# Attention row maxima: both heads' first factors in two row halves of the array, placed on either side of the P @ V batch

## The chip, the cores and the metric

The kernel runs on one core of a Trainium2 chip. The metric is the device time of one execution in microseconds (us). The engines are called as the profile calls them: PE is TensorE (PEld its weight loads), DVE is VectorE, ACT is ScalarE, POOL is GpSimd, SP is SyncE, which here issues all DMAs.

## The reference

For each of 16 images (256 channels, 32 x 32 positions): a group norm, self-attention with 4 heads of 64 channels over 1024 positions, a projection with a residual, and then a residual bottleneck of three convolutions whose weights are mixed from 8 experts per image.

```python
xn = group_norm(x, gn_w, gn_b)
q, k, v = split(einsum('oc,bchw->bohw', qkv_w, xn) + qkv_b[...])   # 4 heads of 64
attn = softmax(einsum('bhdm,bhdn->bhmn', q, k) / sqrt(64), axis=-1)
x = x + einsum('oc,bchw->bohw', proj_w, einsum('bhmn,bhdn->bhdm', attn, v)) + proj_b
rw = sigmoid(x.mean(axis=(2, 3)) @ router_w.T + router_b)
# conv 1x1 (256->64), conv 3x3 (64->64), conv 1x1 (64->256), weights einsum('be,e...->b...', rw, experts)
out = relu(conv3(relu(bn(conv2(relu(bn(conv1(x))))))) + x)
```

The softmax needs a number for each query that lies near the maximum of its row of scores; any such number gives the same result, since it cancels.

## The kernel before

Queries and keys are kept split into a first part (fp32r) and a small rest. `Q1[:, h]` holds the first part of head h's queries in both 64-partition halves; `K1[:, h]` holds the first part of the keys in one half and the rest in the other, so that a product over 128 partitions is q1 times (k1 + k2). `Q2` and `K2` hold the rest and, in one row, the negated row maxima with a row of ones.

An image is worked off as follows: a block is a pair of heads and a half of the queries (4 blocks), a step is one tile of 128 keys of a block (8 steps a block, 32 an image), a turn is two steps (`TURNS` = 16 an image). On PE a turn t is: the scores `S` of one step (`scores`, four matmuls, L541 and L544), the jobs of the table `MID` for this turn, the scores of the next step, the jobs of `LATE`, then both steps' P @ V products (`pv`, L557), then the jobs of `HALVES`. All jobs (QKV tiles, projections, convolutions, group-norm sums) share one PSUM bank, `SB`. ACT takes the exponential of each score tile and drains most banks, POOL adds up the probabilities, DVE reduces maxima, splits q and k, normalises and mixes the experts.

The row maxima are made one block ahead. A fill (`max_fill`, L522) writes the scores of 128 queries against all 1024 keys of one head into `MS` (two banks), two matmuls of 128 rows each; a `reduce_max` on DVE (L738) takes them down to one column of `mx`. `MS` exists once, so each fill waits on `max_read` for the reduce of the fill before it. A block has 8 fills (2 heads x 4 query tiles), a turn has 2: one after each step's scores. When a block's 8 columns are there, the job "row" (turns 2, 6, 10, 14; L470) transposes and negates them on PE, DVE copies them to `mrow` (L742), and SP sends them into `Q2`, where the block's scores need them (`rows_loaded`).

Each engine's program is written out in the same turn order and runs in that order; semaphores join them. So a PE instruction that waits holds all of PE behind it. `section` is emitted for images 0, 1, a loop body over images 2 to 14, and image 15; image 15 makes no fills after its own blocks.

## Time and profile before

| | |
|---|---|
| median of 3 runs | 2131.06 us (2130.21 to 2134.96) |
| the profiled execution | 2136.77 us, of which the span of the trace is 2135.0 us |
| busy share of the span | PE 92%, DVE 75%, POOL 52%, ACT 49%, PEld 50% |
| granted TensorE clock, mean | 0.988 |
| chain that ended last | PE 72%, DVE 17%, issue 8% |
| one image in the middle (turn 14 to turn 14) | 129.5 us |

A row of the profile's groups gives the line, engine and operation, what is written from what, the shapes, the count, then the busy time and the mean of one, then how long the engine sat idle just before and who ended the idle time. PE records last until a modelled end and overlap; the time from one start to the next is what a matmul costs in a stream.

### The profile page before, as it was taken

What the parts mean: (1) busy time and instruction counts of PE and PEld (TensorE: products, weight loads), DVE (VectorE), ACT (ScalarE), POOL (GpSimd) and SP (SyncE); (2) the same over time, 40 slices, a digit from 0 to 9 for tenths busy, and PEclk for the clock granted to TensorE, in tenths of its full rate; (3) what the DMA queues carried; (4) which work ended last, traced back from release to release, by engine and by line L of the source; (5) the groups of instructions that cost most, each with busy time, mean ns of one, the idle gap of its engine ahead of it and who ended that gap; (6) DMA issues with size and microseconds to landing.
All of it is one profiled execution on the core that took longest, in us unless ns stands there. A gap on an engine that the chain in (4) does not pass through costs nothing.

```text
span 2135.0 us, 26026 instructions
## 1 busy us (share of the span) xinstructions
PE 1960.0 (92%) x8072; PEld 1058.0 (50%) x8072; DVE 1598.7 (75%) x1750; ACT 1047.3 (49%) x1346; POOL 1112.6 (52%) x485
## 2 busy tenths in 40 slices
PE   5899899999999999899998999989999998999986
PEld 4455554545545445454454554545454554544532
DVE  5768868687785967959688686877859689596665
ACT  3554545454455454554445454544554545544432
POOL 2665545464564545545555554545645555455551
PEclk9999999999999999999999999999999999999998
DMA  4002120111202012020121201112020120201101
GB/s 150 21 21 70 26 89 21 48 47 25 89 20 86 8 35 79 20 94 10 30 74 25 89 17 42 55 25 89 20 85 10 35 79 20 94 10 30 54 6 65
DMA packets 44189, 102.02 MB, mean 48 GB/s; under 512 B 7168, under 2 KB 7936, under 8 KB 44032
## 3 DMA queue, kind: packets, MB, share of 16 engines
q1 hardware_dynamic: 44160, 101.65, 15.6%
q8 instruction: 16, 0.26, 0.1%
q14 instruction: 13, 0.11, 0.0%
HBM read 37.91 MB, written 16.78 MB: 26 GB/s over the span
## 4 chain that ended last, share of the span: by engine, by line
PE 72%; DVE 17%; issue 8%; ACT 2%; DMA 1%; DVEq 0%; SPq 0%; POOL 0%; ACTq 0%
PE PV L557 17%; PE SB L428 11%; PE S L541 9%; PE MS L522 9%; PE S L544 7%; DVE mx L738 5%; PE SB L465 5%; PE SB L499 4%; DVE rz L807 3%; PE SB L507 3%; PE SB L459 3%; DVE mix L830 2%; PE SB L486 2%; DVE gsc L721 1%; DVE bst L715 1%
## 5 line engine op out<-in xcount | busy, mean ns | idle before, releaser
L414 POOL TENSOR_TENSOR psum_p<-psum_p,prob 128x1024 f32<-128x1024 f32 x384 | 933.0, 2430 | 658.5 <-ACT prob L620 652.4
L738 DVE TENSOR_REDUCE mx<-MS 128x1 f32<-128x1024 f32 x500 | 604.3, 1209 | 312.6 <-PE MS L522 309.3
L620 ACT ACTIVATE prob<-S 128x1024 f32<-128x1024 f32 x512 | 523.6, 1023 | 383.1 <-PE S L544 380.8
L557 PE MATMUL PV<-prob,V 128*64 128x512 f32 x2048 | 503.1, 613 | 0.0
L541 PE MATMUL S<-Q,K 128*128 128x512 f32 x1024 | 457.2, 446 | 3.0 <-DVE mx L887 3.0
L544 PE MATMUL S<-Q,K 128*128 128x512 f32 x1024 | 404.1, 395 | 0.0
L522 PE MATMUL MS<-K,Q 128*128 128x512 f32 x1000 | 330.0, 411 | 68.2 <-DVE mx L738 68.2
L541 PEld LDWEIGHTS S<-Q,K 128*128 128x128 f32 x1024 | 192.8, 188 | 261.6 <-issue 217.3
L414 POOL TENSOR_TENSOR psum_p<-prob 128x1024 f32<-128x1024 f32 x64 | 154.3, 2411 | 308.4 <-ACT prob L620 308.4
L557 PEld LDWEIGHTS PV<-prob,V 128*64 128x64 f32 x2048 | 125.9, 138 | 262.4 <-issue 238.6
L522 PEld LDWEIGHTS MS<-K,Q 128*128 128x128 f32 x1000 | 175.5, 189 | 159.7 <-DVE mx L738 130.0
L807 DVE RECIPROCAL rz<-rz 128x256 f32<-128x256 f32 x128 | 222.7, 1740 | 3.2 <-ACT rz L649 2.3
L544 PEld LDWEIGHTS S<-Q,K 128*128 128x128 f32 x1024 | 193.8, 189 | 38.0 <-issue 10.8
L775 DVE TENSOR_TENSOR K<-qk_raw,K 64x512 fp32r<-64x512 f32 x128 | 107.0, 836 | 85.8 <-ACT K L638 84.9
L775 DVE TENSOR_TENSOR Q<-qk_raw,Q 64x512 fp32r<-64x512 f32 x128 | 124.7, 974 | 50.1 <-ACT Q L638 49.2
L634 ACT ACTIVATE qk_raw<-SB,vec 128x512 f32<-128x512 f32 x124 | 85.4, 689 | 81.8 <-PE SB L428 80.7
L830 DVE SCALAR_TENSOR_TENSOR mix<-ex,rw,mix 128x768 f32<-128x768 f32 x105 | 118.7, 1131 | 1.4
L465 PE MATMUL SB<-o,wp 128*128 128x512 f32 x240 | 112.7, 592 | 0.0
L625 ACT ACTIVATE o<-PV 128x512 f32<-128x512 f32 x64 | 38.3, 598 | 141.3 <-PE PV L557 141.3
L428 PE MATMUL SB<-x_hi,w_hi 128*128 128x512 f32 x248 | 98.7, 398 | 4.3 <-DVE x_lo L730 4.3
L428 PE MATMUL SB<-x_lo,w_hi 128*128 128x512 f32 x248 | 98.1, 395 | 0.0
L428 PE MATMUL SB<-x_hi,w_lo 128*128 128x512 f32 x248 | 97.9, 395 | 0.0
(126 smaller groups left out, 1929.7 us busy)
## 6 DMA issues: line engine op xcount, KB each, us to landing
xin<-in_x_dram SPq DMA_DIRECT2D x16, 1024.0 KB, 6.5
K<-K SPq DMA_DIRECT2D x128, 128.0 KB, 2.3
Q<-Q SPq DMA_DIRECT2D x128, 128.0 KB, 2.2
x<-in_x_dram SPq DMA_DIRECT2D x16, 1024.0 KB, 5.1
out_dram<-y SPq DMA_DIRECT2D x64, 256.0 KB, 2.0
V<-v_next SPq DMA_DIRECT2D x16, 512.0 KB, 4.4
hpad<-hpad SPq DMA_DIRECT2D x16, 289.0 KB, 3.1
ex<-in_experts_dram SPq DMA_DIRECT2D x1, 3072.0 KB, 11.9
```

The costliest lines, as they stand in the source:

```text
L414: nc.gpsimd.tensor_tensor(acc, first_in, prob[:, s % PBUF, :, :], ALU.add).then_inc(add_done, 1)
L428: last = nc.tensor.matmul(dst, wl(w, c), xl(m, c), start=(k == 0), stop=(k == 3 * CC - 1))
L465: last = nc.tensor.matmul(bank, wp[:, c, oc * P:oc * P + P], o[:, c, px(hf)], start=(c == 0), stop=(c == CC - 1))
L522: last = nc.tensor.matmul(MS[:, nh, :], Q1[:, h, q0:q0 + P], K1[:, h, px(nh)], start=True, stop=True)
L541: nc.tensor.matmul(S[:, s % 2, a, :], K1[:, h, kt * P:kt * P + P], Q1[:, h, px(hf)], start=True, stop=False)
L544: last = nc.tensor.matmul(S[:, s % 2, a, :], K2[:, h, kt * P:kt * P + P], Q2[:, h, px(hf)], start=False, stop=True)
L557: last = nc.tensor.matmul(PV[own(a), :], V[:, b // NH, kt, a * D:a * D + D], prob[:, s % PBUF, a, :], start=(kt == 0), stop=(kt == KT - 1))
L620: nc.scalar.activation(prob[:, s % PBUF, :, :], S[:, s % 2, :, :], ACT.Exp, scale=D ** -0.5).then_inc(exp_done, 1)
L738: nc.vector.reduce_max(mx[:, b % 2, m:m + 1], MS[:, :, :], AX.XY).then_inc(max_read, 1)
L775: last = nc.vector.tensor_tensor(dst, qk_raw[own(a), f % 2, :], hi[own(a), h, px(hf)].bitcast(F32), ALU.subtract)
L807: nc.vector.reciprocal(rz[:, f % 2, cols], rz[:, f % 2, cols]).then_inc(rz_ready, 1)
L830: nc.vector.scalar_tensor_tensor(out=mix[:, :], in0=ex[:, e, :], scalar=rw[:, e:e + 1], in1=mix[:, :], op0=ALU.mult, op1=ALU.add).then_inc ...
```

## The change

A fill now writes both heads' scores for 128 queries and one half (512) of the keys: head a's matmul uses only the 64 partitions that hold its first parts (`own(a)`: rows 0 to 63 of the array for head 0 of the pair, rows 64 to 127 for head 1) and writes bank a of `MS`. The rest of the keys is left out of the maximum. There are still 8 fills a block and 2 a turn. In PE's program both leave their places behind the scores: one stands directly before the turn's P @ V products, the other behind these and the `HALVES` job. In DVE's program both reduces stand together behind the `LATE` jobs of the turn. A reduce now gives two columns (one for each head), for one key half; a ninth, small reduce for each block takes the larger of the two halves, and `row` waits for that one (`max_ready`).

```diff
-        mx = sb("mx", [P, 2, 2 * QT])
+        mx = sb("mx", [P, NH, 2, QT])
+        mx1 = sb("mx1", [P, 2 * QT])
...
-                    pe.wait_ge(max_read, 8 * (BLOCKS * i + f + 1))
-                    last = nc.tensor.matmul(bank[0:2 * QT, 0:P], mx[:, f % 2, :], negeye[:, :], start=True, stop=True)
+                    pe.wait_ge(max_ready, BLOCKS * i + f + 1)
+                    last = nc.tensor.matmul(bank[0:2 * QT, 0:P], mx1[:, :], negeye[:, :], start=True, stop=True)
...
                 pe.wait_ge(max_read, 32 * i + 8 * b + m)
-                q0 = hf * HALF + m % QT * P
-                for nh in range(NH):
-                    last = nc.tensor.matmul(MS[:, nh, :], Q1[:, h, q0:q0 + P], K1[:, h, px(nh)], start=True, stop=True)
+                q0 = hf * HALF + t * P
+                for a in range(2):
+                    last = nc.tensor.matmul(MS[:, a, :], Q1[own(a), 2 * p + a, q0:q0 + P], K1[own(a), 2 * p + a, px(nh)],
+                                            start=True, stop=True)
                 last.then_inc(max_filled, 1)
...
                             scores(i + 1, half)
-                        at = fill_at(i, 2 * t + half, last)
-                        if at:
-                            max_fill(*at)
                         for kind, di, f in jobs_of(place, t, first, last):
                             job(kind, i + di, f, held)
                             held = [(kind, i + di, f)]
+                    at = fill_at(i, 2 * t, last)
+                    if at:
+                        max_fill(*at)
                     pv(i, 2 * t)
                     pv(i, 2 * t + 1)
                     for kind, di, f in jobs_of(HALVES, t, first, last):
                         job(kind, i + di, f, [] if kind == "conv2" else held)
                         held = [(kind, i + di, f)]
+                    at = fill_at(i, 2 * t + 1, last)
+                    if at:
+                        max_fill(*at)
...
+            def max_of(g, b, m, banks):
+
+                dve.wait_ge(max_filled, g + 1)
+                nc.vector.reduce_max(mx[:, m % NH, :, m // NH], banks, AX.X).then_inc(max_read, 1)
+
+            def max_of_block(i, b):
+                dve.wait_ge(max_read, 32 * i + 8 * b + 8)
+                wait(dve, filled["row"], BLOCKS * i + b)
+                nc.vector.reduce_max(mx1[:, :], mx[:, :, :, :].rearrange("p n a t -> p (a t) n"), AX.X).then_inc(max_ready, 1)
+
             def max_reduce(i, b, m):
-                n = 32 * i + 8 * b + m + 1
                 if m == 0:
-                    wait(dve, filled["row"], BLOCKS * i + b - 1)
-                dve.wait_ge(max_filled, n)
-                nc.vector.reduce_max(mx[:, b % 2, m:m + 1], MS[:, :, :], AX.XY).then_inc(max_read, 1)
+                    wait(dve, max_ready, BLOCKS * i + b)
+                max_of(32 * i + 8 * b + m, b, m, MS[:, :, :])
+                if m == 7:
+                    max_of_block(i, b)
...
                     for half, place in ((0, MID), (1, LATE)):
-                        at = fill_at(i, 2 * t + half, last)
-                        if at:
-                            max_reduce(*at)
                         for kind, di, f in jobs_of(place, t, first, last):
                             job(kind, i + di, f)
+                        if half == 1:
+                            for n in (2 * t, 2 * t + 1):
+                                at = fill_at(i, n, last)
+                                if at:
+                                    max_reduce(*at)
```

The twelve fills ahead of image 0 (`max_fill_pair`) change in the same way and stay where they are.

On PE, in turn 7 of the loop body (a turn without jobs), the end of the turn before the change reads as follows; L544 is the last of the turn's scores, L522 the fill, L557 the P @ V products, L541 the next turn's first scores.

```order
L544 MATMUL S<-Q,K 128x512
L519 REGISTER_ALU
L522 MATMUL MS<-K,Q 128x512 [waits max_read]
L522 MATMUL MS<-K,Q 128x512
L557 MATMUL PV<-prob,V 64x512 [waits exp_done]
L557 MATMUL PV<-prob,V 64x512
L557 MATMUL PV<-prob,V 64x512 [waits exp_done]
L557 MATMUL PV<-prob,V 64x512
L541 MATMUL S<-Q,K 128x512 [waits exp_done]
```

After the change (L546, L523, L559 and L543 are the same operations) it reads:

```order
L546 MATMUL S<-Q,K 128x512
L520 REGISTER_ALU
L523 MATMUL MS<-K,Q 128x512 [waits max_read]
L523 MATMUL MS<-K,Q 128x512
L559 MATMUL PV<-prob,V 64x512 [waits exp_done]
L559 MATMUL PV<-prob,V 64x512
L559 MATMUL PV<-prob,V 64x512 [waits exp_done]
L559 MATMUL PV<-prob,V 64x512
L520 REGISTER_ALU
L523 MATMUL MS<-K,Q 128x512 [waits max_read]
L523 MATMUL MS<-K,Q 128x512
L543 MATMUL S<-Q,K 128x512 [waits exp_done]
```

The fill that stood behind the turn's first scores (not in these rows) has gone, one stands before the P @ V products and one stands behind them, each with its wait for the reduce of the fill before.

On DVE, in turn 9 of the loop body (a QKV job for Q in `MID` and one in `LATE`), the order before is this; L738 is the reduce of a fill, L775 the split of q for a head.

```order
L738 TENSOR_REDUCE mx<-MS 128x1 [waits max_filled]
L773 ISA
L775 TENSOR_TENSOR Q<-qk_raw,Q 64x512 [waits qk_hi]
L773 REGISTER_ALU
L775 TENSOR_TENSOR Q<-qk_raw,Q 64x512 [waits qk_hi]
L737 REGISTER_ALU
L738 TENSOR_REDUCE mx<-MS 128x1 [waits max_filled]
L773 ISA
L775 TENSOR_TENSOR Q<-qk_raw,Q 64x512 [waits qk_hi]
L773 REGISTER_ALU
L775 TENSOR_TENSOR Q<-qk_raw,Q 64x512 [waits qk_hi]
```

And after (L741 is the reduce, L790 the split):

```order
L788 ISA
L790 TENSOR_TENSOR Q<-qk_raw,Q 64x512 [waits qk_hi]
L788 REGISTER_ALU
L790 TENSOR_TENSOR Q<-qk_raw,Q 64x512 [waits qk_hi]
L788 ISA
L790 TENSOR_TENSOR Q<-qk_raw,Q 64x512 [waits qk_hi]
L788 REGISTER_ALU
L790 TENSOR_TENSOR Q<-qk_raw,Q 64x512 [waits qk_hi]
L740 REGISTER_ALU
L741 TENSOR_REDUCE mx<-MS 128x2 [waits max_filled]
L740 REGISTER_ALU
L741 TENSOR_REDUCE mx<-MS 128x2 [waits max_filled]
```

The reduce that stood ahead of the `LATE` job's two splits, and the one ahead of the `MID` job's, now stand behind all four.

The third place is PE between turn 9 and turn 10 after the change, where the row job (L472) comes: the fill (L523) that completes a block stands behind the P @ V products, four score matmuls further on the row job waits for `max_ready`. Before the change a fill of the next block lay between the scores and the row job, and the block's last fill stood ahead of the P @ V products.

```order
L520 REGISTER_ALU
L523 MATMUL MS<-K,Q 128x512 [waits max_read]
L523 MATMUL MS<-K,Q 128x512
L543 MATMUL S<-Q,K 128x512 [waits exp_done]
L546 MATMUL S<-Q,K 128x512
L543 MATMUL S<-Q,K 128x512
L546 MATMUL S<-Q,K 128x512
L437 REGISTER_ALU
L472 MATMUL SB<-negeye,mx 8x128 [waits max_ready,qk_read]
```

The row job's wait is now for the ninth reduce of the block that the fill a few rows above completes.

## Rows read from the trace of the kernel before

**Rows 1.** The page's costliest groups: a fill's reduce and the reciprocal, on DVE.

```profile
L738 DVE TENSOR_REDUCE mx<-MS 128x1 f32<-128x1024 f32 x500 | 604.3, 1209 | 312.6 <-PE MS L522 309.3
...
L807 DVE RECIPROCAL rz<-rz 128x256 f32<-128x256 f32 x128 | 222.7, 1740 | 3.2 <-ACT rz L649 2.3
```

**Rows 2.** Windows, one a turn: 0, 1, 3, 6, 7, 8, 9, 11, and all 16 (length first, then each engine's busy time, PEclk, DMA).

```profile
944.01:952.72 8.71, 8.71 (x39) 5.12 (x37) 6.19 (x8) 6.55 (x9) 5.38 (x3) 1.00 0.84 324
952.72:960.67 7.95, 7.95 (x32) 4.53 (x31) 6.23 (x7) 4.60 (x6) 4.40 (x3) 1.00 0.29 66
...
967.99:975.61 7.62, 6.96 (x29) 3.71 (x27) 7.05 (x11) 2.05 (x2) 2.19 (x1) 1.00 0.00 0
...
989.19:995.09 5.90, 5.61 (x24) 2.60 (x22) 5.76 (x10) 4.65 (x5) 4.31 (x3) 1.00 0.00 1
995.09:1002.72 7.63, 5.38 (x22) 2.50 (x20) 7.63 (x7) 3.86 (x4) 4.79 (x2) 1.00 0.00 0
1002.72:1012.17 9.45, 8.96 (x39) 5.04 (x37) 7.65 (x8) 6.55 (x9) 5.10 (x2) 1.00 0.12 28
1012.17:1019.85 7.68, 7.68 (x34) 4.83 (x32) 6.60 (x8) 6.05 (x9) 4.05 (x3) 1.00 0.30 68
...
1028.29:1038.39 10.10, 8.21 (x43) 4.65 (x41) 9.62 (x9) 3.31 (x5) 2.48 (x1) 1.00 0.00 0
...
sum 129.50, PE 121.11 PEld 65.44 DVE 99.39 ACT 65.27 POOL 68.86; mean PE 7.57 PEld 4.09 DVE 6.21 ACT 4.08 POOL 4.30
```

**Rows 3.** Timeline of PE, turn 9 and the start of turn 10 (start, us, engine, line).

```profile
1012.17 0.50 PE L541 MATMUL S<-Q,K 128*128 128x512 f32 x1
...
1013.20 0.62 PE L522 MATMUL MS<-K,Q 128*128 128x512 f32 x2
1013.66 0.40 PE L428 MATMUL SB<-x_hi,w_hi 128*128 128x512 f32 x1
...
1015.06 0.40 PE L541 MATMUL S<-Q,K 128*128 128x512 f32 x1
...
1015.99 0.68 PE L522 MATMUL MS<-K,Q 128*128 128x512 f32 x2
...
1017.67 0.39 PE L428 MATMUL SB<-x_hi,w_lo 128*128 128x512 f32 x1
1017.99 1.94 PE L557 MATMUL PV<-prob,V 128*64 128x512 f32 x8
1019.85 0.50 PE L541 MATMUL S<-Q,K 128*128 128x512 f32 x1
1020.19 0.40 PE L544 MATMUL S<-Q,K 128*128 128x512 f32 x1
```

**Rows 4.** Timeline of PE's weight loads where a fill had waited.

```profile
1024.34 0.30 PEld L522 LDWEIGHTS MS<-K,Q 128*128 128x128 f32 x2 [1.81 <-DVE mx L738]
1024.68 0.19 PEld L428 LDWEIGHTS SB<-w_hi,x_hi 128*128 128x128 f32 x1
```

**Rows 5.** Timeline of ACT, turn 9's LATE QKV job.

```profile
1018.35 0.69 ACT L634 ACTIVATE qk_raw<-SB,vec 128x512 f32<-128x512 f32 x1
```

**Rows 6.** Timeline of DVE, turns 7 to 9.

```profile
1000.06 2.63 DVE L730 TENSOR_TENSOR x_lo<-xin,x_hi 128x1024 fp32r<-128x1024 f32 x1
...
1016.65 1.60 DVE L775 TENSOR_TENSOR Q<-qk_raw,Q 64x512 fp32r<-64x512 f32 x2 [0.77 <-ACT Q L638]
...
1019.73 2.38 DVE L775 TENSOR_TENSOR Q<-qk_raw,Q 64x512 fp32r<-64x512 f32 x2 [0.22 <-ACT Q L638]
```

**Rows 7.** Waits of PE, whole span (total, times, longest).

```profile
PE SB L507 <- DVE mrow L742: 16.7, 14, 1.3
```

**Rows 8.** Timeline of PE in image 1's turn 7.

```profile
220.53 0.74 PE L522 MATMUL MS<-K,Q 128*128 128x512 f32 x2 [2.07 <-DVE mx L738]
221.21 3.42 PE L557 MATMUL PV<-prob,V 128*64 128x512 f32 x8
```

**Rows 9.** Windows, a piece of the same turn.

```profile
222.50:225.00 2.50, 2.50 (x7) 0.69 (x4) 2.50 (x3) 0.34 (x1) 0.00 (x0) 0.51 0.00 0
```

17 lines of the change are left out of this document (10 added, 7 removed).

## Prediction

> **What bounds the kernel now.** I read the page's busy shares first, then the chain that ended last, then one image in the middle turn by turn with windows, then PE, DVE and ACT in the timeline of single turns. PE is busy 121.11 of an image's 129.5 us, DVE 99.39 [rows 2]. In most turns PE runs without a gap; where it stops, it is for DVE. So a microsecond that PE issues less, or waits less, is a microsecond, and because PE's program is one queue, a PE instruction that waits for DVE costs its whole wait. DVE has 30 us free in an image, but not everywhere: in turn 7 it is busy for all 7.63 us and PE for 5.38, in turn 6 for 5.76 of 5.90 [rows 2].
>
> From the starts of the records (a stream of these fp32r matmuls starts one each 0.23 us) I took what of each turn is waiting: turn 0 0.2, turn 1 0, turn 3 0.8 (for statistics), turn 6 0.55, turn 7 2.8, turn 8 0.95 (for the split of x), turn 9 0.05, turn 11 2.0 (conv1 for the expert mix), turn 15 0; the other seven turns together 4.1, of which 1.2 is conv3 in turn 14 waiting for the copy of the maxima [rows 7]. In all 11.5 us an image.
>
> **The change part by part: the fills.** A fill costs 0.46 us today: its matmuls start at 1013.20, the next job's at 1013.66 [rows 3]. Its weights load behind other matmuls and cost nothing. Two a turn are 0.93. The trace has no matmul of 64 rows, but it shows what a change between 128 and 64 columns costs. Into P @ V: the last matmul before it starts at 1017.67, would end its turn in the stream at 1017.90, and P @ V starts at 1017.99, so 0.09 is lost. Out of it: eight records at 0.22 each end at 1019.76, the scores' weights start at 1019.85 (0.09), and the first score matmul is followed after 0.34 instead of 0.23, because its weight load (0.11) has nothing to hide behind [rows 3]. The same 0.11 stands where a fill had waited: fill's first load at 1024.34, next job's load at 1024.68, which is 0.11 and one matmul of 0.23 [rows 4].
>
> The new fill always stands between two forms. It pays 0.09 to get in and its own first weight load, 0.11. If the two row halves then run side by side, the second's load follows the first's (0.11) and its matmul ends 0.23 later: 0.09 + 0.11 + 0.11 + 0.23 = 0.54. The way out was paid before as well, by the P @ V batch. Bounds: with both loads side by side too, 0.43; if the halves run one after the other, 0.09 + 0.11 + 2 x 0.23 = 0.66. I take 0.54, since one weight load after another is what these rows show. Fills then cost 1.08 a turn instead of 0.93: +0.15, or +2.4 us an image. The halved array work is eaten by the changes of form.
>
> The Trainium skill (TensorEngine Tiling, Key Properties) says that changing the tiling mode drains TensorE and that tiles execute weight loads and matmuls in parallel. The lost 0.09 of [rows 3] agrees with the first half; by the second the low bound, 0.43, would hold and the fills would save 1 us an image.
>
> **The reduces.** Their count stays, their duration too (1.21 us, [rows 1]; input of the same shape; two results instead of one). The ninth reduce reads 16 columns; small DVE operations of the trace lie between 0.15 and 0.3, so four an image cost DVE about 1 us.
>
> What counts is the new place. Fill B (behind P @ V) may start only when the reduce of fill A (in front) is through, as `MS` is one buffer; that reduce stands behind all DVE work of the turn's MID and LATE jobs; and behind fill B on PE are the next turn's scores, on which ACT, POOL and everything else live. P @ V covers 1.87 us [rows 3], a reduce needs 1.21 and about 0.05 for its semaphore. So DVE must be free within 0.6 us of fill A's end. Let P be when PE would reach fill B, counted from the turn's start, and A when the reduce is through; the turn then takes max(P, A) + 0.54. P is the turn's old length less its waits, less 0.93, plus 0.54. The first scores take 1.03, a QKV job 1.40, the second scores 0.93 [rows 3].
>
> Turn 9: the LATE job's two splits end at 1019.73 + 2.38 = 1022.11, 9.94 after the turn's start [rows 6]. They hang on ACT, which comes to this job only at 1018.35 [rows 5], after the MID job's copies and an exponential. One fill (0.46) less ahead of it: 9.48, so A = 10.75. P = 7.68 - 0.05 - 0.93 + 0.54 = 7.24. PE waits 3.5. Before, the reduces stood ahead of these splits, and nothing waited. Turn 0 is the same with a z job of 0.9: P = 8.1, wait 2.6. Turn 8 too: 2.65, and see below.
>
> Turns 15 and 1: the MID splits end 3.2 after their PE job (1018.25 against 1015.06, [rows 3, 6]), so at 2.43 + 3.2 = 5.6; then a reciprocal (1.74, [rows 1]), in turn 1 a projection's 0.75: A = 8.5 and 9.3, P = 7.25 and 7.55. Waits 1.25 and 1.7.
>
> Turns 6 to 8: DVE is full. Into turn 6 it carries fill B's reduce, the block's reduce, and the affine step; free at 3.4, then copy, reciprocal, mix: A = 7.45, P = 5.3, wait 2.15. Into turn 7 it carries 3.8; then a split of x, 2.63 beside POOL [rows 6]: A = 7.65, P = 4.5, wait 3.2. In turn 8 the first QKV job waits 1.35 for the second split of x.
>
> Turn 3: PE comes to the statistics' matmul two fills earlier, DVE does not: 2.0; then 0.7 for the reduce behind the variance. Turn 11: conv1 stands at the end of DVE's mix chain, now one reduce longer ahead: 2.9.
>
> Row jobs (turns 2, 6, 10, 14): the block's last reduce now starts when fill B ends; 1.21 + 0.05 + 0.25 for the block's own reduce against 1.12 of scores: 0.35 each. In turn 14 the copy no longer stands behind a reduce: conv3's 1.2 becomes 0.45.
>
> **The sum.** Waits after in the nine turns named, in their order: 2.6 + 1.7 + 2.7 + (0.35 + 2.15) + 3.2 + (1.35 + 2.65) + 3.5 + 2.9 + 1.25 = 24.35, before 7.35: +17.0. The other seven: about 2.4 after, 4.1 before (what PE waited at fills in turns 5 and 10 goes, since fill A now has scores and jobs between it and the reduce it waits for): -1.7. With the fills +2.4: +17.7 us an image. Image 15 makes few fills and has no QKV jobs, image 0 no old jobs; I count 15 images: +265.
>
> **The clock.** In image 1's turn 7 PE waited those 2.07 us for the reduce, and then P @ V took 3.42 instead of 1.94; the granted clock was 0.51, the level of 1.2 GHz [rows 8, 9]. In the image of rows 2 the same wait ended at 1.00, the level of 2.4 GHz. Of the 14 images with this wait I find the fall in six (windows of 5 us over the whole span). A fall costs 1.5 us. After the change seven waits an image are 2 us or longer, three of them 2.9 or more. I count two falls an image on the path (some fall where DVE is what everybody waits for): 2 x 1.5 x 15 = +45.
>
> 265 + 45 = +310. The profiled execution (2136.77 us, span 2135.0) lies 0.3% over the median, and that much doesn't show here; on the median of 2131: **2440 us**.
>
> The Trainium skill (TensorE: Matmul & The Clock Gate, Why this matters for your kernels) advises against idle gaps of more than about 3 us between bursts; by it only turns 7 and 9 would fall, which gives the same two an image, while [rows 8] show falls from shorter gaps.
>
> **The rivals.**
> *No falls of the clock*: for it, eight of 14 images today. 2131 + 265 = 2396. Chance 0.15.
> *A fall at nearly each long wait*: six an image, +135: 2530. For it, the waits grow from 2.1 to over 3. Chance 0.13.
> *Row halves give all they promise*: 0.24 a fill with no way in or out. All fills B and the fills A of the seven turns where PE sets the length gain 0.3: 23 x 0.3 x 15 = -104, so 2336. Against it, the 0.09 and 0.11 of [rows 3]. Chance 0.13.
> *The halves don't run side by side* (the change doesn't do what it says): 23 x 0.12 x 15 = +41, 2480. Chance 0.14.
> *Faster*: DVE keeps up. With 99 us of work in 129 [rows 2] it has room; if ACT comes to the LATE jobs earlier, since fewer fills lie ahead, and the splits end within 0.6 us of fill A, the new waits vanish with the old 4 us at the fills: -4 and +2.4 an image, with the fill at its low bound -5, so 2131 - 75 = 2056 at best. It decides where the DVE end of the LATE splits falls under 5.9 us of the turn; I have 9.5, and 7.6 would still cost 1.6. Chance 0.03.
>
> **How the numbers follow.** My own case, with the rest of 0.42, is 2440, and its size is uncertain by a third of the waits, since each turn's DVE backlog is an estimate from the one before: 2350 to 2510. The range reaches to 2315 for the concurrent halves, and 2525 for the clock: about 0.8. 0.2% is what a measurement of this kernel tells from no change. Slower 0.95, same 0.02, faster 0.03.
>
> **What the profile after would show.** An image of about 150 us; POOL and DVE shares down, PE's busy share near 85%. Waits of PE at the fill for the reduce: from 68 us to over 250, most of them at fill B in turns 0, 7, 8, 9, over 3 us the longest. The row matmul waiting for DVE some 0.35 us, 60 times. Fill matmuls starting about 0.11 apart, 0.54 from the end of the scores to P @ V. A mean granted clock near 0.96. I'm wrong if the LATE splits end early, if fill A's reduce finds DVE free, or if PE's waits at fill B are taken back from its other waits.

## The result, and the profile after

The changed kernel takes 2405.43 us (median of 4, 2401.08 to 2409.14) against 2133.01 for the kernel before in the same rounds: 1.128 times as long (95% interval 1.125 to 1.130). Slower, as forecast, 35 us under the forecast time and inside the range.

The page of the changed kernel: the span, the engines, the chain by engine, and the two groups that answer to [rows 1].

```profile
span 2405.0 us, 26141 instructions
...
PE 2009.8 (84%) x8072; PEld 1009.6 (42%) x8072; DVE 1574.3 (65%) x1814; ACT 1047.7 (44%) x1346; POOL 1100.0 (46%) x485
...
PE 52%; DVE 25%; issue 14%; ACT 8%; DVEq 1%; DMA 0%; POOL 0%; ACTq 0%; SPq 0%; POOLq 0%
...
L741 DVE TENSOR_REDUCE mx<-MS 128x2 f32<-128x1024 f32 x504 | 614.7, 1220 | 373.7 <-PE MS L523 370.1
...
L523 PE MATMUL MS<-K,Q 64*128 64x512 f32 x1000 | 256.5, 510 | 225.2 <-DVE mx L741 225.2
```

PE's matmuls are busy hardly longer than before, but their share of the span is 84% for 92%. In the chain PE has 52% (72% before) and DVE 25% (17%). The fills (L523) now name PE's wait for the reduce as 225.2 us of idle matmul time, 68.2 before.

One image in the middle, a window a turn, as [rows 2]; shown are turns 0, 1, 3, 6, 7, 8, 9, 10, 11 and the sum of all 16 (length, then busy time of PE, PEld, DVE, ACT and POOL, then PEclk).

```profile
1362.34:1373.68 11.34, 8.69 (x38) 4.74 (x36) 7.28 (x7) 6.55 (x9) 4.75 (x2) 1.00 0.63 220
1373.68:1384.51 10.83, 9.61 (x33) 5.22 (x31) 6.07 (x7) 4.00 (x5) 4.73 (x2) 0.84 0.10 24
...
1392.09:1402.54 10.45, 7.20 (x28) 3.26 (x26) 8.38 (x14) 2.65 (x3) 2.36 (x1) 1.00 0.00 0
...
1415.35:1422.69 7.34, 5.43 (x24) 2.30 (x22) 6.55 (x11) 5.83 (x6) 5.77 (x3) 1.00 0.00 1
1422.69:1428.31 5.62, 4.84 (x22) 2.28 (x20) 5.02 (x5) 3.29 (x4) 3.37 (x2) 1.00 0.00 0
1428.31:1441.13 12.82, 8.94 (x39) 4.67 (x37) 10.35 (x8) 6.54 (x9) 5.34 (x3) 1.00 0.18 41
1441.13:1452.41 11.28, 7.76 (x34) 4.45 (x33) 7.92 (x7) 5.95 (x8) 4.82 (x2) 1.00 0.20 47
1452.41:1460.67 8.26, 8.24 (x36) 4.65 (x35) 5.42 (x6) 2.71 (x4) 4.75 (x2) 0.79 0.00 0
1460.67:1472.97 12.30, 9.53 (x42) 4.50 (x40) 9.50 (x8) 3.92 (x6) 2.35 (x1) 0.88 0.00 0
...
sum 146.77, PE 124.38 PEld 62.14 DVE 98.15 ACT 65.33 POOL 67.63; mean PE 7.77 PEld 3.88 DVE 6.13 ACT 4.08 POOL 4.23
```

An image takes 146.8 us instead of 129.5. Turns 0, 1, 3, 8, 9 and 11 grew by 2.2 to 3.6 us each, turn 6 by 1.4 and turn 15 by 1.2; turn 7, in which DVE had been full, shrank by 2.0.

Turn 9's end on PE (L523 fill, L559 P @ V, L543 scores):

```profile
1446.10 0.49 PE L523 MATMUL MS<-K,Q 64*128 64x512 f32 x2
1446.52 1.94 PE L559 MATMUL PV<-prob,V 128*64 128x512 f32 x8
1451.98 0.50 PE L523 MATMUL MS<-K,Q 64*128 64x512 f32 x2 [3.52 <-DVE mx L741]
1452.41 0.50 PE L543 MATMUL S<-Q,K 128*128 128x512 f32 x1
...
1453.02 0.63 PE L543 MATMUL S<-Q,K 128*128 128x512 f32 x1
```

Fill A stands at 1446.10, P @ V 0.42 behind it. Fill B then waits 3.52 us, and only 0.43 after its start come the scores. The score records behind it are 0.63 long where 0.39 is the length at full clock: the clock has fallen. DVE shows what the fill waited for:

```profile
1423.95 0.68 DVE L827 TENSOR_TENSOR o<-o,rz 128x512 f32<-128x512 f32 x1
...
1425.47 1.22 DVE L735 TENSOR_TENSOR x_lo<-xin,x_hi 128x1024 fp32r<-128x1024 f32 x1
...
1448.24 2.43 DVE L790 TENSOR_TENSOR Q<-qk_raw,Q 64x512 fp32r<-64x512 f32 x2 [1.03 <-ACT Q L643]
1450.70 1.23 DVE L741 TENSOR_REDUCE mx<-MS 128x2 f32<-128x1024 f32 x1
```

The LATE job's two splits (L790) run from 1448.24 to 1450.67, the reduce of fill A starts behind them at 1450.70 and ends at 1451.93, and fill B starts at 1451.98. Fill A had been complete since 1446.6. (The first two rows, of turn 7, are used further down.)

### The profile page after: what moved, and what is told of

Same layout as the page of the kernel before. It is cut to its first block, busy times and chain, and to the rows that moved or that the text cites. A ratio compares the mean times of both kernels' runs of the same rounds, so it can differ in the third digit from the quotient of the medians.

```text
span 2405.0 us, 26141 instructions
## 1 busy us (share of the span) xinstructions
PE 2009.8 (84%) x8072; PEld 1009.6 (42%) x8072; DVE 1574.3 (65%) x1814; ACT 1047.7 (44%) x1346; POOL 1100.0 (46%) x485
## 4 chain that ended last, share of the span: by engine, by line
PE 52%; DVE 25%; issue 14%; ACT 8%; DVEq 1%; DMA 0%; POOL 0%; ACTq 0%; SPq 0%; POOLq 0%
DVE mx L741 9%; PE PV L559 9%; PE S L543 8%; PE SB L430 7%; PE MS L523 7%; PE S L546 6%; PE SB L467 3%; ACT qk_raw L639 3%; PE SB L501 3%; DVE mix L845 3%; PE SB L509 3%; PE SB L488 2%; DVE rz L822 2%; ACT K L643 2%; ACT Q L643 2%
## 5 line engine op out<-in xcount | busy, mean ns | idle before, releaser
L416 POOL TENSOR_TENSOR psum_p<-psum_p,prob 128x1024 f32<-128x1024 f32 x384 | 915.2, 2383 | 919.6 <-ACT prob L625 911.8
L741 DVE TENSOR_REDUCE mx<-MS 128x2 f32<-128x1024 f32 x504 | 614.7, 1220 | 373.7 <-PE MS L523 370.1
L559 PE MATMUL PV<-prob,V 128*64 128x512 f32 x2048 | 496.3, 605 | 0.0
L543 PE MATMUL S<-Q,K 128*128 128x512 f32 x1024 | 480.1, 469 | 3.1 <-DVE mx L741 3.1
L523 PE MATMUL MS<-K,Q 64*128 64x512 f32 x1000 | 256.5, 510 | 225.2 <-DVE mx L741 225.2
L546 PE MATMUL S<-Q,K 128*128 128x512 f32 x1024 | 423.5, 414 | 0.4 <-DMA Q<-mrow 0.4
L523 PEld LDWEIGHTS MS<-K,Q 64*128 64x128 f32 x1000 | 95.2, 187 | 555.0 <-DVE mx L741 400.1
L543 PEld LDWEIGHTS S<-Q,K 128*128 128x128 f32 x1024 | 203.8, 199 | 127.9 <-issue 92.9
L546 PEld LDWEIGHTS S<-Q,K 128*128 128x128 f32 x1024 | 207.0, 202 | 41.5 <-issue 10.8
L559 PEld LDWEIGHTS PV<-prob,V 128*64 128x64 f32 x2048 | 124.5, 136 | 211.4 <-issue 179.2
L790 DVE TENSOR_TENSOR Q<-qk_raw,Q 64x512 fp32r<-64x512 f32 x128 | 128.4, 1003 | 129.3 <-ACT Q L643 128.4
L790 DVE TENSOR_TENSOR K<-qk_raw,K 64x512 fp32r<-64x512 f32 x128 | 114.3, 893 | 122.4 <-ACT K L643 119.9
L845 DVE SCALAR_TENSOR_TENSOR mix<-ex,rw,mix 128x768 f32<-128x768 f32 x105 | 161.9, 1541 | 1.0
L430 PE MATMUL SB<-x_hi,w_hi 128*128 128x512 f32 x248 | 111.5, 450 | 21.3 <-DVE x_lo L735 21.3
L467 PE MATMUL SB<-o,wp 128*128 128x512 f32 x240 | 116.2, 607 | 13.2 <-DVE o L827 13.2
L488 PE MATMUL SB<-x,mix 128*64 128x512 f32 x128 | 48.5, 893 | 46.4 <-DVE mix L850 42.4
```

The costliest lines, as they stand in the source:

```text
L416: nc.gpsimd.tensor_tensor(acc, first_in, prob[:, s % PBUF, :, :], ALU.add).then_inc(add_done, 1)
L430: last = nc.tensor.matmul(dst, wl(w, c), xl(m, c), start=(k == 0), stop=(k == 3 * CC - 1))
L467: last = nc.tensor.matmul(bank, wp[:, c, oc * P:oc * P + P], o[:, c, px(hf)], start=(c == 0), stop=(c == CC - 1))
L523: last = nc.tensor.matmul(MS[:, a, :], Q1[own(a), 2 * p + a, q0:q0 + P], K1[own(a), 2 * p + a, px(nh)], start=True, stop=True)
L543: nc.tensor.matmul(S[:, s % 2, a, :], K1[:, h, kt * P:kt * P + P], Q1[:, h, px(hf)], start=True, stop=False)
L546: last = nc.tensor.matmul(S[:, s % 2, a, :], K2[:, h, kt * P:kt * P + P], Q2[:, h, px(hf)], start=False, stop=True)
```

## The experiments

All times are medians; ratios are against the kernel before on the same chip, with their 95% intervals. The kernel before has a median of 2131.1 to 2134.4 us on these chips, so a difference between two experiments is good to some 3 us. Where it is said in how many images the clock fell, images 1 to 14 of the profiled execution are meant.

**1. The reduce of fill A ahead of the LATE job's DVE work.** The changed kernel, DVE only.

```diff
+                        if half == 1:
+                            at = fill_at(i, 2 * t, last)
+                            if at:
+                                max_reduce(*at)
                         for kind, di, f in jobs_of(place, t, first, last):
                             job(kind, i + di, f)
                         if half == 1:
-                            for n in (2 * t, 2 * t + 1):
-                                at = fill_at(i, n, last)
-                                if at:
-                                    max_reduce(*at)
+                            at = fill_at(i, 2 * t + 1, last)
+                            if at:
+                                max_reduce(*at)
```

> The changed kernel, with one line moved on DVE: the reduce of fill A stands in front of the LATE job's DVE work, the reduce of fill B stays behind it. PE's program is untouched. Theory (PE stands at fill B because the reduce of fill A is queued behind the LATE jobs on DVE): the waits of turns 0, 8 and 9 at fill B (2.6, 2.65, 3.5 us) go, 0.7 each in turns 1 and 3, about two falls of the clock of 1 us go; the row job of turn 10 waits 2 us more, since its block's last reduce still stands behind the LATE splits. About -10 us an image, near 2255 us in all, still slower than before the change. Rival (the form changes of the array in each turn are the cost): PE issues the same matmuls in the same order, so less than 20 us is gained, 2385 or more.

2289.47 us, ratio 1.0725 (1.0701 to 1.0749): 116 us of the 272 come back with PE's program unchanged. PE's wait at the fills falls from 225.2 to 113.9 us. The windows of turns 8 to 11 in this kernel:

```profile
1355.28:1365.57 10.29, 8.89 (x38) 4.66 (x36) 7.33 (x7) 6.27 (x9) 6.18 (x3) 1.00 0.14 32
1365.57:1376.07 10.50, 7.77 (x34) 4.45 (x32) 9.44 (x8) 6.25 (x9) 5.29 (x2) 1.00 0.30 68
1376.07:1386.64 10.57, 9.23 (x36) 5.71 (x34) 6.34 (x8) 2.71 (x4) 5.52 (x2) 0.68 0.00 0
1386.64:1397.56 10.92, 8.15 (x42) 4.27 (x40) 9.50 (x8) 3.64 (x6) 2.35 (x1) 1.00 0.00 0
```

Turn 8 is 2.5 us shorter than in the changed kernel and turn 0 2.7 (8.63). But turns 9 to 11 together are 32.0 us, as in the changed kernel (31.8). I had counted turn 9's 3.5 us as gained, and PE still waits 2.73 us there. DVE's rows and POOL's show why:

```profile
1369.60 4.73 DVE L790 TENSOR_TENSOR Q<-qk_raw,Q 64x512 fp32r<-64x512 f32 x2 [0.93 <-ACT Q L643]
1371.43 2.35 POOL L416 TENSOR_TENSOR psum_p<-psum_p,prob 128x1024 f32<-128x1024 f32 x1 [0.51 <-ACT prob L625]
```

The two splits of the MID job, which stand ahead of the reduce of fill A in this order too, take 4.73 us beside an addition of POOL; in the changed kernel they take 2.05. In turn 10 the row job then waits 1.34 us for the block's last reduce, which still stands behind the LATE splits, and the turn runs at a granted clock of 0.68. The cause is shown, the size I gave it was too large by 34 us.

**2. The new fills in the places of before.** The changed kernel's narrow fills, two-column reduces and ninth reduce; each fill behind a step's scores, each reduce ahead of the job.

```diff
+                        at = fill_at(i, 2 * t + half, last)
+                        if at:
+                            max_fill(*at)
                         for kind, di, f in jobs_of(place, t, first, last):
                             job(kind, i + di, f, held)
                             held = [(kind, i + di, f)]
-                    at = fill_at(i, 2 * t, last)
-                    if at:
-                        max_fill(*at)
...
-                    at = fill_at(i, 2 * t + 1, last)
-                    if at:
-                        max_fill(*at)
...
+                        at = fill_at(i, 2 * t + half, last)
+                        if at:
+                            max_reduce(*at)
                         for kind, di, f in jobs_of(place, t, first, last):
                             job(kind, i + di, f)
-                        if half == 1:
-                            for n in (2 * t, 2 * t + 1):
-                                at = fill_at(i, n, last)
-                                if at:
-                                    max_reduce(*at)
```

> The new fills (both heads in two row halves) and the ninth reduce, but in the places of before: one fill behind each step's scores, its reduce ahead of the job's DVE work. Theory: a fill in the midst of 128-row matmuls pays a change of form on both sides, 0.09 in, 0.44 to the next load, 0.11 for that load: 0.64 instead of 0.46 in about 29 of 32 fills an image, some of it under waits for DVE: +60 us, near 2195. Waits of PE for the reduce near the 68 us of before. Rival (the new places are innocent, the narrow form is what costs): most of the 272 us are there, 2350 or more. Second rival (row halves are a gain by themselves): at or under 2133.

2179.09 us, ratio 1.021 (1.019 to 1.023). So the places cost 226 us of the 272, and the narrow form in the midst of wide matmuls 46, with all that it sets off. A fill there, on PE:

```profile
1297.60 0.40 PE L546 MATMUL S<-Q,K 128*128 128x512 f32 x1
1297.92 0.51 PE L523 MATMUL MS<-K,Q 64*128 64x512 f32 x2
1298.36 0.50 PE L430 MATMUL SB<-x_hi,w_hi 128*128 128x512 f32 x1
1298.70 0.39 PE L430 MATMUL SB<-x_lo,w_hi 128*128 128x512 f32 x1
```

The last score matmul starts at 1297.60 and would be followed at 1297.83; the fill comes at 1297.92 (0.09 lost), the job's first load 0.44 later, and its second matmul 0.34 behind the first instead of 0.23 (0.11 lost). 0.64 in all, against 0.46 for the wide fill of [rows 3].

This price alone is not the 46 us. In turn 13, where PE waits for nothing, two fills make 7.75 us of 7.42, 0.17 each. But turns 7 and 8 together take 19.1 us in 12 of 14 images, where they took 17.1, or 17.7 with a fall of the clock: the waits at turn 7's fills are 2.5 us for 2.25, and the clock now falls in all 14 images instead of six. The two turns in the kernel before, in an image with the fall, and here:

```profile
1254.07:1263.29 9.22, 6.98 (x22) 3.00 (x21) 9.22 (x8) 3.85 (x4) 4.78 (x2) 0.81 0.00 0
1263.29:1271.77 8.48, 8.48 (x38) 5.20 (x36) 6.25 (x7) 6.55 (x9) 4.48 (x2) 1.00 0.13 31
...
1144.54:1154.18 9.64, 7.12 (x22) 2.62 (x20) 9.64 (x8) 4.00 (x4) 4.99 (x2) 0.72 0.00 0
1154.18:1163.65 9.47, 9.47 (x38) 5.15 (x36) 6.07 (x7) 6.54 (x9) 4.64 (x2) 0.92 0.12 28
```

About half of the 46 us lies in these two turns. The clock, which I had not named as a rival, has its part in it.

**3. The fills of before in the new places.** The other half alone: the kernel before, its 128-row fills and its reduces moved as the change moves them.

```diff
-                        at = fill_at(i, 2 * t + half, last)
-                        if at:
-                            max_fill(*at)
                         for kind, di, f in jobs_of(place, t, first, last):
                             job(kind, i + di, f, held)
                             held = [(kind, i + di, f)]
+                    at = fill_at(i, 2 * t, last)
+                    if at:
+                        max_fill(*at)
                     pv(i, 2 * t)
                     pv(i, 2 * t + 1)
...
+                    at = fill_at(i, 2 * t + 1, last)
+                    if at:
+                        max_fill(*at)
...
-                        at = fill_at(i, 2 * t + half, last)
-                        if at:
-                            max_reduce(*at)
                         for kind, di, f in jobs_of(place, t, first, last):
                             job(kind, i + di, f)
+                        if half == 1:
+                            for n in (2 * t, 2 * t + 1):
+                                at = fill_at(i, n, last)
+                                if at:
+                                    max_reduce(*at)
```

> The fills of before (one head, 128 rows, both key halves, no ninth reduce) in the new places on PE and DVE. Theory: the places cost it all; a fill is 0.46 instead of 0.44, the row job doesn't wait for a ninth reduce (-0.2 four times an image): 2395 to 2420, and PE's waits for the reduce as long as in the changed kernel. Rival (narrow form costs): the time falls to below 2250.

2429.96 us, ratio 1.1385 (1.1362 to 1.1408), with a granted clock of 0.950 (0.955 in the changed kernel). PE's waits of this kernel are those of the changed one:

```profile
PE MS L522 <- DVE mx L741: 223.5, 123, 4.1
```

Without any narrow matmul the loss is all there and 25 us more, 10 above the range I gave. In turns 5 and 13, where PE waits for nothing, a wide fill costs 0.04 us more than a narrow one (5.31 us for 5.23, 7.61 for 7.54), so in these places the narrow form is a small gain; the larger part of the 25 us is in turn 9, where the clock fell in 10 of the 14 images (12.7 to 13.2 us) and, in the changed kernel, in one.

**4. Each fill issued twice.**

```diff
-                for a in range(2):
+                for a in (0, 1, 0, 1):
                     last = nc.tensor.matmul(MS[:, a, :], Q1[own(a), 2 * p + a, q0:q0 + P], K1[own(a), 2 * p + a, px(nh)],
```

> The changed kernel with every fill in the loop issued twice over (four matmuls, the second pair writes the same scores again). Theory (the two halves and their weight loads run side by side): a pair more costs 0.23 us; on the path are all fills B and the fills A of the seven turns in which PE sets the length, 23 x 0.23 x 15 = +80 us, near 2485. Rival (the halves run one after the other and what looks short is the modelled record): 0.46 a pair, +160, near 2565.

2477.33 us, ratio 1.1614 (1.1589 to 1.1638): +72 us for 500 pairs more, 0.14 each on average and near 0.2 for those on the path (turn 5, where PE alone sets the length, grows from 5.23 to 5.68, 0.23 a fill). The total also holds falls of the clock that moved: turn 1 has none here (10.26 for 10.83), turn 9 has one in nearly every image (12.8 to 13.3 for 11.3). The turns in which PE waits for nothing give the price by itself. The row halves do run at the same time; one after the other they would have cost 0.46.

**5 to 7. Single moves in the kernel before.** Five: only its second fill moved on PE, to behind the LATE job, in front of P @ V. Six: only DVE's copy of the row maxima put ahead of the reduce. Seven: both.

```diff
                         at = fill_at(i, 2 * t + half, last)
-                        if at:
+                        if at and half == 0:
                             max_fill(*at)
                         for kind, di, f in jobs_of(place, t, first, last):
                             job(kind, i + di, f, held)
                             held = [(kind, i + di, f)]
+                        if at and half == 1:
+                            max_fill(*at)
```

```diff
                         at = fill_at(i, 2 * t + half, last)
+                        jobs = jobs_of(place, t, first, last)
+                        for kind, di, f in jobs:
+                            if kind == "row":
+                                job(kind, i + di, f)
                         if at:
                             max_reduce(*at)
-                        for kind, di, f in jobs_of(place, t, first, last):
-                            job(kind, i + di, f)
+                        for kind, di, f in jobs:
+                            if kind != "row":
+                                job(kind, i + di, f)
```

> The kernel of before with only its second fill moved on PE: behind the LATE job, in front of P @ V, as fill A of the change stands, in the old form of 128 rows. DVE's order is as before: each reduce ahead of the LATE job's work. Theory (only the place behind P @ V and the reduces' place behind the LATE jobs cost time, the place in front of P @ V is good): the LATE job's PE work now covers the wait for the reduce before; turn 10 gains 1.3 of its 1.65 us, turns 0 and 4 0.2 and 0.4: -1.9 us an image, near 2106. Rival (each move of a fill towards P @ V makes a later reduce and so a wait): 2150 or more. No fill changes its form, so nothing is to be had or lost there.

> The kernel of before with one exchange on DVE: in turns 2, 6, 10 and 14 the copy of the row maxima stands ahead of the reduce instead of behind it, as it does in the changed kernel. Theory: conv3 in turn 14, which waits 1.2 us for the copy, waits 0.3 (as 0.4 in the changed kernel), while in turns 6 and 10 the reduce comes 0.2 later and its fill with it: -0.8 us an image, near 2120. Rival: the delayed reduce costs as much as the copy gains, 2130 to 2140.

> Both moves together. If they are independent: -2.7 us an image, near 2093; if the delayed reduce of the one eats the cover of the other, no better than the first alone.

Five: 2183.51 us, ratio 1.0241 (1.0227 to 1.0255), 51 us slower where I expected 26 faster. My theory that the place in front of P @ V is good fell. Its waits of PE:

```profile
PE MS L522 <- DVE mx L740: 41.9, 51, 2.1
...
PE SB L438 <- DVE bst L717: 26.4, 16, 8.9
PE SB L428 <- DVE mrow L744: 21.5, 15, 1.5
```

The wait at the fill did shrink, from 68.2 to 41.9. It came back one place further on: DVE's order was left as it was, so the reduce of the fill that now comes later stood ahead of the LATE job's drain of `SB`, and of the group norm's statistics. The statistics' matmul waits 26.4 instead of 18.7, and a QKV job waits 21.5 for the copy of the row maxima, a wait that the kernel before did not have. Turns 3, 4 and 13 are 0.5 to 0.9 longer, and turns 7 and 8 together, with a fall of the clock in turn 7 in 11 of 14 images, take 17.9 to 18.0, where the kernel before takes 17.1, or 17.7 to 17.8 in its six images with the fall.

Six: 2135.31, ratio 1.0014 (1.0005 to 1.0023). Conv3's wait fell from 16.7 to 6.4 us as expected and turn 14 by 0.7, but turns 2 and 6 took it back (+0.67, +0.28): the rival. Seven: 2173.62, ratio 1.0195 (1.0181 to 1.0209), 10 us better than five alone and no gain.

**8. The first experiment, with LATE QKV splits behind both reduces.**

```diff
+                        jobs = jobs_of(place, t, first, last)
...
-                        for kind, di, f in jobs_of(place, t, first, last):
-                            job(kind, i + di, f)
+                        for kind, di, f in jobs:
+                            if half == 0 or kind != "qk":
+                                job(kind, i + di, f)
...
+                            for kind, di, f in jobs:
+                                if kind == "qk":
+                                    job(kind, i + di, f)
```

> The changed kernel with the reduce of fill A in front of the LATE job's DVE work (the first experiment, 2289 us) and, in the three turns with a LATE QKV job, the reduce of fill B too. Theory: the row job of turn 10, which there waited 2.3 us for a reduce behind the splits, waits 0.35, and fill A of turns 1 and 9 isn't held by a late reduce of fill B: -3 us an image, near 2240, the rest over 2133 being the DVE backlog of turns 6 to 8, turn 11's mix chain, turn 3 and falls of the clock. Rival (what is left over 2133 hangs on the splits' end, wherever the reduces stand): 2275 to 2295.

2306.86 us, ratio 1.0819 (1.0802 to 1.0835): 17 us slower than the first, where 50 faster was expected; nearest to the rival. Windows of turns 9, 10, 11:

```profile
1370.07:1381.00 10.93, 7.77 (x34) 4.45 (x32) 10.21 (x7) 6.24 (x9) 5.36 (x2) 1.00 0.28 65
1381.00:1389.51 8.51, 8.47 (x36) 4.62 (x34) 6.81 (x8) 2.71 (x4) 5.14 (x2) 0.80 0.00 0
1389.51:1402.09 12.58, 9.81 (x42) 4.55 (x41) 9.50 (x8) 3.63 (x6) 2.46 (x2) 0.86 0.00 0
```

Turn 10's row wait did go (8.51 for 10.57), and turn 11 is longer (12.58 for 10.92). It has no new wait: conv1 waits 2.77 us for the mix in both kernels, and only here does the clock fall after it. In the first experiment and in this one:

```profile
1395.26 1.94 PE L488 MATMUL SB<-x,mix 128*64 128x512 f32 x8 [2.77 <-DVE mix L850]
...
1398.13 3.60 PE L488 MATMUL SB<-x,mix 128*64 128x512 f32 x8 [2.77 <-DVE mix L850]
```

PE's wait at fill B of turn 9 is 3.16 us, after 2.73 in the first experiment and 3.52 in the changed kernel. The three turns are 32.0 us in this image, 32.0 in the first experiment and 31.8 in the changed kernel, and 26.2 before. That they agree so well is chance: in other images of this run they take 30.7 us, where turn 11 has no fall of the clock, or 35.6, where turn 10 is at a clock of 0.72 and waits 2.0 more for the copy of the maxima. None of these orders of the reduces brings them near 26.2.

**9. The expert mix of turn 10 ahead of the reduces,** in the changed kernel.

```diff
+                        early = 0
+                        if half == 1 and t == 10 and not first:
+                            early = MIX_LATE[t]
+                            mix_experts(i - 1, mixed, mixed + early)
+                            mixed += early
                         if half == 1:
                             for n in (2 * t, 2 * t + 1):
...
-                        if count and not first:
+                        if count and not first and not early:
```

> The changed kernel with one exchange on DVE, in turn 10 alone: the two steps of the expert mix stand ahead of the two reduces instead of behind. In the changed kernel DVE idles 1.73 us before the first of these reduces and 1.07 before the second, since their fills come late, and the mix that conv1 of turn 11 waits for is queued behind. Theory (a second price of the new place: DVE itself waits for late fills with the mix chain behind it): the mix runs in that gap, conv1 comes about 1.5 us earlier, -1.5 us an image or 22 us in all, near 2383; with the fall of the clock in turn 11 gone too, near 2368. Rival (conv1 hangs on the reciprocal and the steps of turn 11 whatever stands before): 2400 or more.

2403.49 us, ratio 1.1261 (1.1236 to 1.1287): no change. The number is the rival's, the reason is not. Conv1's wait is gone (turn 11 is 9.46 for 12.30) and turn 10 has it (11.15 for 8.26). The mix steps on DVE, with the reduce behind them:

```profile
1455.20 4.92 DVE L845 SCALAR_TENSOR_TENSOR mix<-ex,rw,mix 128x768 f32<-128x768 f32 x2
1460.05 1.21 DVE L741 TENSOR_REDUCE mx<-MS 128x2 f32<-128x1024 f32 x1
```

The two steps took 4.92 us here and 2.06 in the changed kernel, so the reduce of fill A was 2.3 late at fill B. POOL's additions lay beside them (last section).

**10. The first fill of a turn in front of the scores,** in the kernel before: directly behind P @ V, in the wide form, its reduce still ahead of the MID job, the other fill unmoved.

```diff
+                        at = fill_at(i, 2 * t + half, last)
+                        if at and half == 0:
+                            max_fill(*at)
                         if t < TURNS - 1:
                             scores(i, 2 * t + 2 + half)
                         elif not last:
                             scores(i + 1, half)
-                        at = fill_at(i, 2 * t + half, last)
-                        if at:
+                        if at and half == 1:
                             max_fill(*at)
```

> The kernel of before with one exchange on PE: the turn's first fill stands in front of its first scores, so directly behind P @ V of the turn before, as fill B of the change; in the old form of 128 rows, DVE's order as before, the other fill behind the second scores. Theory (the place behind P @ V is innocent as long as the reduce that it waits for stands ahead of the LATE jobs on DVE): the fill waits for a reduce that P @ V covers, and the next fill has the scores more between: waits in turns 4 to 7 shrink a little, where DVE is full they stay: 2110 to 2145. Rival (a fill behind P @ V costs by itself, since it stands ahead of the scores that ACT needs): 2170 or more.

2138.38 us, ratio 1.0022 (1.0012 to 1.0032). The place behind P @ V costs next to nothing in sum, with DVE's order left as it was. It isn't free of waits: at the fills PE waits 107.9 us over the span, for 68.2 before. Turns 15, 0 and 1 together are 2.4 us longer; conv3's wait for the copy of the maxima (6.4 us over the span, 16.7 before), some tenths each in turns 2, 4, 5 and 11, and a turn 7 without a fall of the clock in any image give it back.

**11. The same in the second experiment,** so with narrow fills, one directly behind P @ V and one behind the second scores. PE only, against the second experiment.

```diff
+                        at = fill_at(i, 2 * t + half, last)
+                        if at and half == 0:
+                            max_fill(*at)
                         if t < TURNS - 1:
...
-                        at = fill_at(i, 2 * t + half, last)
-                        if at:
+                        if at and half == 1:
                             max_fill(*at)
```

> The new fills with the places of before (the second experiment, 2179 us), except that the turn's first fill stands directly behind P @ V, in front of the first scores, as in the experiment before this one. Theory (a narrow fill costs 0.44 us where the form changes anyway and 0.64 amid 128-row matmuls): 16 fills an image come down by 0.2, less what lies under waits for DVE: -2.5 to -3 us an image, near 2138. Rival (narrow fills cost the same wherever they stand, the 46 us of the second experiment are the ninth reduce's or the clock's): 2170 or more.

2147.9 us, ratio 1.0086 (1.0069 to 1.0103): 31 us less than the second experiment. Half the fills no longer stand amid wide matmuls, and in turn 13, where PE waits for nothing, that one fill gives back 0.19 us (7.56 for 7.75), as the theory says. But the 31 us are only in part made of this. In turns 7 and 8 the fall of the clock is gone in all 14 images:

```profile
1127.86:1133.86 6.00, 4.86 (x23) 2.28 (x21) 6.00 (x6) 2.40 (x4) 3.33 (x2) 1.00 0.00 0
1133.86:1143.34 9.48, 8.89 (x39) 4.66 (x37) 7.71 (x7) 6.54 (x10) 5.34 (x3) 1.00 0.16 37
```

Part of the wait has moved to turn 6, so I take the three turns together: 23.0 us for 24.9. Turn 14 is 0.7 shorter, since conv3 waits less for the copy. Turns 15, 0 and 1 are 1.7 longer, with waits at the fill behind P @ V. The other nine turns are 1.6 shorter, 0.2 in most of them. Of the 2.6 us that an image gains (130.5 for 133.1), the change of form so makes some 1.6, and the rest is what moved between waits and falls. The rival's number was wrong, but it named the clock, and that is in it. The same places with wide fills are experiment 10: against it the narrow fills, with the ninth reduce, cost 10 to 14 us. So a narrow fill pays its change of form only where there was none before, and what that is worth in the whole kernel can't be read from one total. No version tried beats the kernel before.

## Why the prediction was right, step by step

**The wait of fill B: right, in place and size.** Forecast turn lengths, max(P, A) + 0.54, against measured: turn 0 11.3 and 11.3, turn 8 12.65 and 12.8, turn 9 11.3 and 11.3, turn 15 9.0 and 8.8. The reduce's end in turn 9 was forecast at 10.75 after the turn's start and came at 10.8. Experiment 1 shows that the order on DVE alone makes 116 us of it, experiment 3 that the new places without the narrow form make all of it.

**The price of a fill: the mechanism right, the size too high.** I took 0.54: a change of form (0.09), two weight loads one after the other, a matmul. From the fill's first load to the next instruction's in the other form it is 0.42 to 0.43, a change of form included. That is the low bound of 0.43, with both weight loads side by side: the second load and the second matmul start 0.003 us behind the first, not the 0.11 that the prediction looked for. It is 0.11 a fill less than forecast, some 2.5 us an image over the 23 fills that the prediction takes to be on the path. The Trainium skill (TensorEngine Tiling, Key Properties) says that different tiles can load weights and multiply in parallel; the trace agrees, with these 0.003 us. Against the 0.46 of the wide fill this is a gain of 0.03 in the new places and, by experiment 2, a loss of 0.18 amid wide matmuls.

**DVE's backlog, turns 6 and 7: too high.** Turn 7 was forecast at 8.2 and is 5.6; turn 6 8.0 and 7.3. I had carried the old durations over. In [rows 6] the split of x took 2.63; after the change it took 1.22, and the normalisation (L827) 0.68, because POOL's additions had moved away from them. Turn 3 was forecast at 9.7 and is 10.45: of its waits, the 2.0 before the statistics came as forecast (0.9 at a projection, 1.1 at the statistics), that at fill B was 1.2 for 0.7.

**Turns 9 to 11: right in the sum, but not for one reason.** Experiments 1, 8 and 9 show that the 5.6 us more of these turns do not hang on one place of a reduce. When one wait is removed, DVE's work shifts against POOL's: the MID job's splits went from 2.05 to 4.73 and 3.43 us in experiments 1 and 8, the mix steps from 2.06 to 4.92 in experiment 9. And the clock falls in another place. I had treated the waits as independent and the durations as fixed, which did no harm to the forecast and spoiled the expectations of experiments 1, 5, 8 and 9. How short these three turns could be in the changed places of the fills is open; no run takes away both POOL's share and the falls.

**The clock: right in cost, by luck.** Turns 1, 10 and 11 have windows at 0.84, 0.79 and 0.88 of the level of 2.4 GHz, after waits of 2.65, 3.52 and (conv1 for the mix) 2.8 us. Three falls an image, forecast two. A fall's price in turn 1 can be read from experiment 9, whose turn 1 has the same program and came after a fill's wait as long (2.66) without a fall:

```profile
1371.31:1381.32 10.01, 8.14 (x33) 4.08 (x31) 6.70 (x7) 4.00 (x5) 4.78 (x2) 1.00 0.11 26
```

10.01 at a clock of 1.00 against 10.83 at 0.84: 0.8 us, not the 1.5 that one P @ V batch had suggested; part of a fall lies under the turn's next wait. In turn 10 a fall costs 1.0 to 1.2 (experiment 3: 7.24 us in two images without one, 8.26 to 8.48 in the five at a clock of 0.79 or 0.80). In turn 11 it costs 1.4 (12.30, against 10.92 at 1.00 in experiment 1 with the same wait of 2.77), of which turn 12 gives back 0.2. The three come to about 3 us an image, the forecast's two at 1.5 to the same: the count was too low, the price too high, and that they cancel is luck. The kernel before could have told: its fall makes turn 7 9.2 for 7.6, and turn 8 behind it 8.5 for 9.45, so 0.65 net. The granted clock over the span, forecast near 0.96, is 0.955.

Here the clock fell in turn 1 of all 14 images after that wait of 2.65 us, and in experiment 9 in 8 of 14. The Trainium skill (TensorE: Matmul & The Clock Gate, Why this matters for your kernels) names gaps of more than about 3 us; by these runs shorter ones can be enough, and are not each time.

**Waits that went.** The waits in turns 5 and 10 at the fills did go (turn 10 had one of 1.4 us, turn 5 is 0.3 shorter), and the copy of the maxima is earlier; PE's waits in the changed kernel, as [rows 7]:

```profile
PE MS L523 <- DVE mx L741: 225.2, 123, 5.1
...
PE SB L472 <- DVE mx L746: 25.9, 52, 2.3
...
PE SB L509 <- DVE mrow L757: 6.4, 14, 0.5
```

Conv3 waits 6.4 us for the copy for 16.7 before, and the row job (L472) waits 25.9 us at 52 places, 0.5 each, where 0.35 was forecast. The waits at the fills are 225 us, where the prediction looked for over 250.

The sum: an image was forecast 17.7 + 3 longer and is 17.3, so 3.4 too high, with the falls at about 3 in both. Turns 6 and 7 make 3.2 of it, turn 3 was 0.8 too low; the seven turns without a forecast of their own were some 1.0 too high without turn 10's fall, and turns 0, 1, 8, 9, 11 and 15 lie within 0.3 us each once the falls of turns 1 and 11 are taken out. The price of the fills, 0.11 too high each, is spread over all of them. The mechanism and its size in turns 0, 8 and 9 were right by the working; that the total came within 35 us owes something to errors of opposite sign.

## What to carry to other kernels

When a piece of work is moved on one engine, read its wait from the other engine's queue: what stands ahead of the releasing instruction there decides, not how much room that engine has on average (DVE was 25% idle). A single buffer that is filled twice around a short batch needs its reader to be free within that batch. Before a small difference between two schedules is put down to the price of an instruction, the turns where the engine waits for nothing should be compared by themselves, and the granted clock of the others looked at: experiments 2 and 11 differ by 31 us, and only some 0.6 of this difference is the price that was looked for. Packing a matmul into row halves pays only where the array changes its form anyway; amid full-height matmuls it cost 0.64 us instead of 0.46.

## What the runs showed of the hardware that I had not expected

Two 64-row matmuls of 512 columns with their loads of 128 columns took 0.43 us from the first load to the next form's load, the second load starting 0.003 us behind the first, and a second pair added 0.23.

Some DVE operations, those with both inputs in SBUF among them, and POOL's additions keep each other waiting. POOL in the changed kernel, beside the split of x at 1425.47 to 1426.69:

```profile
1425.94 2.97 POOL L416 TENSOR_TENSOR psum_p<-prob 128x1024 f32<-128x1024 f32 x1 [2.25 <-ACT prob L625]
```

in the kernel before, beside the one that took 2.63 from 1000.06 ([rows 6]):

```profile
999.26 2.35 POOL L414 TENSOR_TENSOR psum_p<-prob 128x1024 f32<-128x1024 f32 x1 [1.74 <-ACT prob L620]
```

and in experiment 9, beside the two mix steps of 1455.20 to 1460.12:

```profile
1453.89 2.38 POOL L416 TENSOR_TENSOR psum_p<-psum_p,prob 128x1024 f32<-128x1024 f32 x1 [6.58 <-ACT prob L625]
1456.43 2.88 POOL L416 TENSOR_TENSOR psum_p<-psum_p,prob 128x1024 f32<-128x1024 f32 x1 [0.15 <-POOL psum_p L416]
```

Where DVE's operation began first it took 1.22 and POOL's 2.97 instead of about 2.4. Where POOL's began first, DVE's ended 1.08 after POOL's end (1001.61), which is nearly its own duration again. The mix steps end 0.8 after the second addition. Over the whole trace of the kernel before, the split of x took 2.25 to 2.78 us in the 15 places where an addition was under way at its start, and 1.21 to 1.23 in the other 17. The fills' reduces, whose input is a PSUM bank, took 1.15 to 1.23 in both cases. The first step of the mix, with one tensor as input (L842 in the changed kernel), took 0.62 in 14 images and 2.60 in the one where an addition was under way. That one holds the other off is read from these times, not tried by itself. It makes durations of such operations depend on where they fall, which is why turn 7 could shrink.
